# Loading the first attention's four head groups inside the projection before it

## The chip, the cores and the metric

The kernel runs on one core of one Trainium2 chip. The metric is the device time of one execution in microseconds. TensorE (PE), VectorE (DVE), ScalarE (ACT), GpSimd (POOL) and SyncE (SP) each run their own instruction stream; SP issues nearly all DMA transfers here, ACT issues a few.

## What is computed

Four blocks with residuals, on x of shape 4 x 1024 x 256. Only the first is touched by the change:

```
x = x + attention(layernorm(x))          # 16 heads of 16, ALiBi bias, causal
x = x + two layers of windowed attention and feed-forward
x = x + a selective scan (Mamba block)
x = x + a top-1 mixture of 32 experts
attention(h): qkv = h @ W_attn + b_attn; att = softmax(q k^T / 4 + alibi + causal); (att @ v) @ W_proj + b_proj
```

## The kernel before, in words

The program is a row of phases. A phase opens its own tiles and semaphores, lets the engines run their streams, and ends with a barrier of all engines at which its semaphores are cleared and its tiles freed. Phases hand data over through tensors in HBM (names `between_...`).

**`phase_qkv`, the projection (tiles `A_...`).** Eight chunks `c` of 512 tokens, two per sequence. For each chunk SP loads `x` (`load`, L255), DVE and POOL normalise it, TensorE transposes it and makes the q, k and value products, ACT puts the products of q and k out as bf16 (`parts`, L381), DVE takes the rest (`rest`, L336), and POOL splits the rest into a second and a third bf16 part (L299, L301). So q and k are each kept as three bf16 parts. `store(c)` on SP writes four value slices (`between_v`, L263) and six part tiles (`between_q_parts`, `between_k_parts`, L269) of 256 KB each. `parts` and `v` have two buffers: before ACT writes the parts of chunk c it waits on `qk_stored`, that is until the parts of chunk c-2 have landed in HBM. On SP the order is: load(c+3), store(c), next chunk. At the end SP waits for all stores, and the phase ends.

**`phase_attention` (tiles `B_...`).** 16 groups `g` = sequence x 4 head groups of four heads, with four buffers (`SETS`) for q, k and values. For a group, six blocks of 16 partitions are filled from the parts of q and six from the parts of k, partition blocks 0 to 95 (L630), rows 96 to 99 hold four extra rows (`q_rows`, `k_rows`), and `v_raw`, `centre` and `key_bias` follow: 17 transfers, about 1.93 MB (12 x 128 KB, 64 KB, 256 KB, 2 x 16 KB). Group 0 is loaded in two halves of its columns by `load_first`, q on SP (L608) and k on ACT (L871), and its values by `values(0)`. SP then issues load(1), load(2), then `put_shift(0)`, the weights, and enters the loop over groups, where load(g+3) comes ahead of what else the group needs.

For group 0 the order of work is strict. TensorE makes 48 score tiles (`p_max`, L911 and L914), DVE takes the maximum of each (L779), then turns them into a shift (L788 to L798), TensorE turns the shift (L935), ACT copies it to `shift_rows` (L880), and SP copies that into rows 96 to 99 of q by four transfers (`put_shift`, L639). Only then may TensorE make the scores that go into the exponential (`p_exp`, L947), with the maxima of the next group woven in between. From there on the shift of a group is made while the group before it is at work.

DVE casts `ident` and `future` at the start of the phase (L767 to L770); both TensorE and DVE wait for their two loads (L602), and TensorE waits for these casts.

`LocalAhead` is an object of the same kind as the new one: tiles of a later phase that are allocated early and loaded by the attention's SP stream.

Of the kernel before, what the change touches and what calls it, by code (L numbers as in the profile page):

```python
# [10 lines left out]
F32 = mybir.dt.float32  # L11
BF16 = mybir.dt.bfloat16
# [186 lines left out]

def phase_qkv(nc, T):
    with ExitStack() as ctx:
        a = Pool_(nc, ctx, "A")
        K = CHUNKS
# [45 lines left out]
        @block.sync  # L251
        def _(sp):
            def load(c):
                reached(sp, xn_ready, c - 2)
                sp.dma_start(x[:, c % 3, :, :], T["x"][c * CHUNK:(c + 1) * CHUNK, :].rearrange("(t p) d -> p t d", p=P)  # L255
                             ).then_inc(x_loaded[c % 3], 16)

            def store(c):
                u, seq, at = c % 2, c // PER_SEQ, c % PER_SEQ * CHUNK
                sp.wait_ge(v_ready, 2 * c + 2)  # L260
                for g in range(GROUPS):
                    row = seq * GROUPS * SEQ + g * SEQ + at
# [197 lines left out]
            "key_bias": seqs(key_bias), "future": np.stack([future, future.T.copy()]), "spread": spread}  # L460


def phase_attention(nc, T, local):
    with ExitStack() as ctx:
        a = Pool_(nc, ctx, "B")
        QB = SEQ // P
# [5 lines left out]
        FIRST = 4  # L472
        LEAD, TURN = 16, 36
        SCORES, PROBS = 3, 12
        SETS = 4
        KR = 100
        stream = [("turn", 0, 0), ("turn", 0, 1)]
        place = {}
        for g in range(NG):
# [11 lines left out]
        ident = a.sb("ident", [P, P])  # L491
        ident_b = a.sb("ident_b", [P, P], BF16)
        future = a.sb("future", [P, 2, P])
        future_b = a.sb("future_b", [P, 2, P], BF16)
        q = a.sb("q", [P, SETS, GH, SEQ], BF16)
        k = a.sb("k", [P, SETS, GH, SEQ], BF16)
        v_raw = a.sb("v_raw", [P, SETS, QB, GW])
        v = a.sb("v", [P, SETS, QB, GH, 32])
        centre = a.sb("centre", [P, SETS, QB * GH])
        key_bias = a.sb("key_bias", [P, SETS, 8, GH])  # L500
# [23 lines left out]
        fixed = a.sem("fixed")  # L524
        cast = a.sem("cast")
        loaded = [a.sem(f"loaded_{b}") for b in range(SETS)]
        v_ready = a.sem("v_ready")
        scored = a.sem("scored")
        maxed = a.sem("maxed")
# [21 lines left out]
        first_half = a.sem("first_half")  # L551
        second_half = a.sem("second_half")
        LOADED = 16 * 17
# [6 lines left out]
        def loaded_by(g):  # L560

            return LOADED * (g // SETS) + (LOADED if g % SETS else 48)

        def part_rows(g, part):
            at = g * GW + part * SEQS * DIM
            return slice(at, at + GW)

        def max_target(g, e):
            at = NE * g + e + 1
# [28 lines left out]

        @block.sync
        def _(sp):  # L600
            for dst, src in ((ident[:, :], T["ident"][:, :]), (future[:, :, :], T["future"].rearrange("a p n -> p a n"))):
                sp.dma_start(dst, src).then_inc(fixed, 16)  # L602

            def load_first():
                for half, done in ((0, first_half), (1, second_half)):
                    cols = slice(512 * half, 512 * half + 512)
                    for n, part in enumerate((0, 0, 1, 1, 0, 2)):
                        sp.dma_start(q[HD * n:HD * n + HD, 0, :, cols], T["q_parts"][part_rows(0, part), cols]  # L608
                                     .rearrange("(h d) t -> d h t", h=GH)).then_inc(done, 16)
                    if half == 0:  # L610
                        sp.dma_start(q[96:KR, 0, :, :], T["q_rows"]).then_inc(done, 16)
                values(0)

            def values(g):
                u = g % SETS
                sem = loaded[u]
                sp.dma_start(v_raw[:, u, :, :], T["v"][g * SEQ:(g + 1) * SEQ, :].rearrange("(t p) d -> p t d", p=P)
                             ).then_inc(sem, 16)
                sp.dma_start(centre[:, u, :], T["centre"][g:g + 1, :].broadcast_to([P, QB * GH])).then_inc(sem, 16)
                sp.dma_start(key_bias[:, u, :, :].rearrange("p a b -> p (a b)"), T["key_bias"][g * P:(g + 1) * P, :]  # L620
                             ).then_inc(sem, 16)

            def load(g):
                u = g % SETS
                sem = loaded[u]
                reached(sp, weighted, STEPS * (g - 3))
                for n, (q_part, k_part) in enumerate(((0, 0), (0, 1), (1, 0), (1, 1), (0, 2), (2, 0))):
                    for x, name, part in ((q, "q_parts", q_part), (k, "k_parts", k_part)):
                        at = g * GW + part * SEQS * DIM
                        sp.dma_start(x[HD * n:HD * n + HD, u, :, :], T[name][at:at + GW, :]  # L630
                                     .rearrange("(h d) t -> d h t", h=GH)).then_inc(sem, 16)
                sp.dma_start(k[96:KR, u, :, :], T["k_rows"][4 * g:4 * g + 4, :, :]).then_inc(sem, 16)
                sp.dma_start(q[96:KR, u, :, :], T["q_rows"]).then_inc(sem, 16)
                values(g)

            def put_shift(g):
                sp.wait_ge(exped, turned[g] + 1)
# [27 lines left out]
                sp.dma_start(T["z"][c * CHUNK + 1:(c + 1) * CHUNK + 1, :].rearrange("(t p) d -> p t d", p=P), z[:, c % 2, :, :]  # L665
                             ).then_inc(z_stored[c % 2], 16)

            load_first()
            load(1)
            load(2)  # L670
            put_shift(0)
            sp.dma_start(w[:, :, :], T["w_proj"].rearrange("(k p) n -> p k n", p=P)).then_inc(w_loaded, 16)
            sp.dma_start(bias[:, :], T["b_proj"].rearrange("(a n) -> a n", a=1).broadcast_to([P, DIM])).then_inc(w_loaded, 16)
            sp.dma_start(T["z"][0:1, :], T["zeros"][0:1, :]).then_inc(first_row, 16)
            for g in range(NG):
                if g + 3 < NG:
                    load(g + 3)
                i, at = divmod(g, GROUPS)
                if at == 2:
# [185 lines left out]

        @block.scalar
        def _(act):
            for half, done in ((0, first_half), (1, second_half)):
                cols = slice(512 * half, 512 * half + 512)
                for n, part in enumerate((0, 1, 0, 1, 2, 0)):  # L870
                    act.dma_start(k[HD * n:HD * n + HD, 0, :, cols], T["k_parts"][part_rows(0, part), cols]  # L871
                                  .rearrange("(h d) t -> d h t", h=GH)).then_inc(done, 16)
                if half == 0:
# [19 lines left out]
        def _(pe):  # L893
# [3 lines left out]
            def score(n):  # L897
# [2243 lines left out]

def build(nc, T):
    with nc.allow_non_contiguous_dma(reason="weights' columns, biases and slots, a few elements each"):
        phase_qkv(nc, T)
        with ExitStack() as outer:
            local = LocalAhead(nc, outer)
            phase_attention(nc, T, local)
            with ExitStack() as inner:
                feed = FeedAhead(nc, inner)
                for layer in range(2):  # L3150
                    phase_window(nc, T, layer, local, feed)
                    phase_feed_forward(nc, T, layer, layer == 1, feed, local)
        phase_front(nc, T)
        phase_scan(nc, T)
        phase_moe(nc, T)
# [21 lines left out]
```

## Time and profile before

| | us |
|---|---|
| median of 3 runs | 3643.21 |
| lowest, highest | 3635.83, 3643.5 |
| span of the profiled execution | 3631.7 |
| busy: PE, DVE, ACT, POOL | 3234.2, 2456.1, 1848.7, 1431.3 |
| projection, its last store landed | about 119 |
| attention, first instruction to first score for the exponential | 120.5 to 173.45 |

The span is counted from the first to the last instruction of the profiled execution; its own device time is not given apart from it. The median of the runs is 11.5 us above the span, and the lowest run 4.1 us above it. The change can move only what lies between the start and the first groups of the attention, so its effect can be read as a shift of a point in the timeline.

### The profile page before, as it was taken

How to read it: one execution, taken by the hardware profiler on the slowest of the kernel's cores; microseconds unless marked ns; L12 is line 12 of the kernel's file. 1: busy time of each engine (PE TensorE's matmuls, PEld its weight loads, DVE VectorE, ACT ScalarE, POOL GpSimd, SP SyncE). 2: the span in 40 equal slices, each digit the busy share in tenths (PEclk: the TensorE clock that was granted, in tenths of full speed). 3: DMA queues.
4: the chain of work that ended last, by engine and by line, in shares of the span. 5: the costliest groups of instructions: out<-in, count | busy, mean ns of one | idle time of the engine just before them, and what ended most of it. 6: DMA issues, size and time to landing. Idle time of an engine off the chain costs nothing. (4 is left out here: it accounts for less than half of the span.)

```text
span 3631.7 us, 52306 instructions
## 1 busy us (share of the span) xinstructions
PE 3234.2 (89%) x18096; PEld 1975.7 (54%) x18096; DVE 2456.1 (68%) x4653; ACT 1848.7 (51%) x3942; POOL 1431.3 (39%) x992
## 2 busy tenths in 40 slices
PE   8599999979999799999999899897388888887798
PEld 5244444346666555566666555332255565555676
DVE  8488887657777522377777232598599999996633
ACT  2177776836666411266666111366377777774100
POOL 4201111132222211132222111244699999995533
PEclk9699999989999899999999899998699999999899
DMA  5945676110020133000200221343615151512873
GB/s 169 161 62 88 78 99 123 28 38 23 23 65 23 51 133 96 22 23 25 67 23 17 69 69 39 101 159 130 240 59 204 58 204 59 203 58 98 296 226 117
DMA packets 276675, 347.29 MB, mean 96 GB/s; under 512 B 71168, under 2 KB 208368, under 8 KB 275772
## 3 DMA queue, kind: packets, MB, share of 16 engines
q1 hardware_dynamic: 261860, 308.29, 30.9%
q10 hardware_dynamic: 9432, 23.35, 1.9%
q0 software_dynamic: 5120, 12.30, 0.9%
q8 instruction: 145, 2.38, 0.3%
q14 instruction: 118, 0.97, 0.1%
HBM read 227.72 MB, written 112.80 MB: 94 GB/s over the span
## 5 line engine op out<-in xcount | busy, mean ns | idle before, releaser
L2373 POOL TENSOR_TENSOR H_feed<-H_ndu,H_bs 128x1024 f32<-128x1024 f32 x256 | 595.3, 2373 | 6.3 <-DMA H_bs<-between_bc 3.2
L888 ACT ACTIVATE B_probs<-B_p_exp,B_key_bias 128x512 f32<-128x512 f32 (+3 forms) x768 | 395.0, 582 | 162.6 <-PE B_p_exp L950 132.2
L779 DVE TENSOR_REDUCE B_part_max<-B_p_max 128x1 f32<-128x512 f32 (+3 forms) x768 | 374.5, 545 | 81.9 <-PE B_p_max L914 79.4
L1298 ACT ACTIVATE D_probs<-D_scores,D_neg,D_rq 128x256 f32<-128x256 f32 x512 | 283.1, 573 | 255.6 <-DVE D_neg L1219 255.6
L2344 ACT ACTIVATE H_decay<-H_ndt,H_rate 128x1024 f32<-128x1024 f32 x256 | 287.8, 1125 | 198.0 <-DVE H_turning L2426 103.2
L1658 PE MATMUL E_p_ag<-E_hT,FA_w 128*128 128x512 f32 x640 | 283.1, 602 | 1.9 <-ACT E_hT L1614 1.9
L911 PE MATMUL B_p_max<-B_k,B_q 100*128 100x512 bf16 (+3 forms) x768 | 256.9, 341 | 29.9 <-DMA B_q<-in_q_rows 20.0
L947 PE MATMUL B_p_exp<-B_q,B_k 100*128 100x512 bf16 (+3 forms) x768 | 250.6, 330 | 23.9 <-DMA B_q<-B_shift_rows 17.1
L2426 DVE TENSOR_TENSOR_SCAN H_turning<-H_decay,H_feed 128x1024 f32<-128x1024 f32 x112 | 253.5, 2274 | 24.1 <-POOL H_feed L2373 22.7
L2477 PEld LDWEIGHTS H_p_y<-H_minus,H_sT 128*128 128x128 f32 x1792 | 224.3, 199 | 76.2 <-ACT H_sT L2329 56.1
L2477 PE MATMUL H_p_y<-H_minus,H_sT 128*128 128x128 f32 x1792 | 232.6, 286 | 35.5 <-ACT H_sT L2329 35.5
L1156 POOL TENSOR_TENSOR D_rnorm<-D_norm,D_power 128x8 f32<-128x8 f32 x64 | 106.1, 1658 | 375.0 <-DVE D_norm L1174 375.0
L1630 ACT ACTIVATE E_gated<-E_p_ag,FA_b 128x512 f32<-128x512 f32 x96 | 62.6, 652 | 372.9 <-PE E_p_ag L1658 353.7
L2329 ACT ACTIVATE H_sT<-H_p_T,H_cT 128x128 f32<-128x128 f32 x896 | 242.9, 387 | 11.7 <-PE H_p_T L2467 11.4
L1353 PE MATMUL D_p_qk<-LA_wqkv,D_hT 128*128 128x512 f32 x512 | 242.3, 617 | 0.9 <-ACT D_hT L1273 0.9
L1216 DVE CUSTOM_DVE_ANT_0 D_scores<-D_scores,D_mask 128x256 f32<-128x256 f32 x512 | 201.9, 457 | 55.0 <-PE D_scores L1380 54.8
L2426 DVE TENSOR_TENSOR_SCAN H_decay<-H_decay,H_feed 128x1024 f32<-128x1024 f32 x96 | 218.9, 2280 | 15.5 <-POOL H_feed L2373 15.5
L1160 POOL TENSOR_TENSOR D_rnorm<-D_norm,D_power 128x8 f32<-128x8 f32 x64 | 106.7, 1667 | 287.7 <-DVE D_norm L1174 287.7
L1658 PEld LDWEIGHTS E_p_ag<-E_hT,FA_w 128*128 128x128 f32 x640 | 121.9, 192 | 155.3 <-issue 151.6
L1585 DVE SCALAR_TENSOR_TENSOR E_act_out<-E_p_ag,FA_b,E_gated 128x512 f32<-128x512 f32 x96 | 67.8, 706 | 198.7 <-ACT E_gated L1630 198.7
L2485 PE MATMUL H_p_y<-H_part,H_minus 128*128 128x512 f32 x384 | 184.5, 603 | 9.6 <-DVE H_part L2402 9.5
L911 PEld LDWEIGHTS B_p_max<-B_k,B_q 100*128 100x128 bf16 x768 | 75.3, 98 | 208.2 <-DVE B_part_max L779 131.4
(269 smaller groups left out, 6858.2 us busy)
## 6 DMA issues: line engine op xcount, KB each, us to landing
H_bs<-between_bc SPq DMA_DIRECT2D x64, 512.0 KB, 8.0
H_cs<-between_bc SPq DMA_DIRECT2D x36, 512.0 KB, 8.5
B_q<-between_q_parts SPq DMA_DIRECT2D x90, 128.0 KB
B_k<-between_k_parts SPq DMA_DIRECT2D x90, 128.0 KB
between_slots_x<-E_clear ACTq DMA_DIRECT2D x4, 2570.0 KB, 18.8
I_xe<-between_slots_x ACTq DMA_DIRECT2D x32, 257.0 KB, 3.9
LA_base<-between_z SPq DMA_DIRECT2D x64, 128.0 KB, 2.2
between_z<-D_z SPq DMA_DIRECT2D x64, 128.0 KB, 1.7
```

Source lines behind the costliest of these rows:

```text
L779: nc.vector.reduce_max(part_max[:, g % 2, kc, qb, h:h + 1], p_max[:, use % 3, 0:keys], AX.X).then_inc(maxed, 1)
L888: nc.scalar.activation(probs[:, x % PROBS, skip:512], p_exp[:, n % SCORES, skip:512], ACT.Exp, bias=key_bias[:, g % SETS, kb - 4 * Q + 4, ...
L911: last = nc.tensor.matmul(p_max[:, use % 3, 0:keys], q[0:KR, u, h, qb * P:(qb + 1) * P], k[0:KR, u, h, 512 * kc:512 * kc + keys], start=Tr ...
L947: last = nc.tensor.matmul(p_exp[:, n % SCORES, skip:512], k[0:KR, u, h, kb * P:(kb + 1) * P], q[0:KR, u, h, 512 * Q + skip:512 * Q + 512], ...
L1298: last = nc.scalar.activation(probs[:, place[m], :, :].rearrange("p a b -> p (a b)"), scores[:, place[m], :, :].rearrange("p a b -> p (a b ...
L1353: last = nc.tensor.matmul(p_qk[:, m, :], hT[:, i % 2, k, :], wqkv[:, k, m * INNER:(m + 1) * INNER], start=k == 0, stop=k == KD - 1)
L1658: last = nc.tensor.matmul(p_ag[:, m % 2, n, :], w1[:, k, at:at + P], hT[:, i % 2, k, :], **flags)
L2329: last = nc.scalar.activation(sT[:, k % 2, h * HB + b, :], p_T[:, h, b, :], ACT.Copy, scale=cT[:, i % 2, h * HB + b, s:s + 1])
L2344: nc.scalar.activation(decay[:, n % 2, :], ndt[:, g % 2, :], ACT.Exp, scale=rate[:, m, s:s + 1]).then_inc(decayed, 1)
L2373: nc.gpsimd.tensor_tensor(feed[:, n % AHEAD, :], ndu[:, g % 2, :], bs[:, s, :], ALU.mult).then_inc(fed, 1)
L2426: nc.vector.tensor_tensor_scan(out, decay[:, n % 2, :], feed[:, n % AHEAD, :], 0.0, ALU.mult, ALU.add).then_inc(scanned, 1)
L2477: last = nc.tensor.matmul(p_y[:, h, b * P:(b + 1) * P], sT[:, k % 2, h * HB + b, :], minus[:, :], start=False, stop=False)
```

## The change

The tiles q, k, v_raw, centre, key_bias, ident and future, with their semaphores, move into an object `AttentionAhead` (tiles `BA_...`), which is open during the projection too. The projection's SP stream loads the two fixed tables at its start and the four first groups after the stores of chunks 3, 4, 5 and 6. The attention's SP stream starts with `put_shift(0)`. Group 0 is no longer loaded in halves, ACT issues no transfer in the attention, and TensorE waits for all 17 transfers of group 0.

```diff
@@ phase_qkv, block.sync
             load(1)
             load(2)
+            first.load_fixed(sp, T)
             for c in range(K):
                 if c + 3 < K:
                     load(c + 3)
                 store(c)
+                if c == 3:
+                    for u in range(2):
+                        sp.wait_ge(qk_stored[u], 96)
+                        sp.wait_ge(v_stored[u], 16 * GROUPS)
+                if 3 <= c < 3 + first.SETS:
+                    first.load(sp, T, c - 3)
@@ new
+class AttentionAhead:
+    SETS, KR = 4, 100
+    LOADED = 16 * 17
...
+    def load_fixed(self, sp, T):
+        sp.dma_start(self.ident[:, :], T["ident"][:, :]).then_inc(self.fixed, 16)
+        sp.dma_start(self.future[:, :, :], T["future"].rearrange("a p n -> p a n")).then_inc(self.fixed, 16)
+
+    def load(self, sp, T, g):
+        u = g % self.SETS
+        sem = self.loaded[u]
+        for n, (q_part, k_part) in enumerate(((0, 0), (0, 1), (1, 0), (1, 1), (0, 2), (2, 0))):
+            for x, name, part in ((self.q, "q_parts", q_part), (self.k, "k_parts", k_part)):
+                at = g * GW + part * SEQS * DIM
+                sp.dma_start(x[HD * n:HD * n + HD, u, :, :], T[name][at:at + GW, :]
+                             .rearrange("(h d) t -> d h t", h=GH)).then_inc(sem, 16)
...
@@ phase_attention, block.sync
             def load(g):
-                u = g % SETS
-                sem = loaded[u]
-                reached(sp, weighted, STEPS * (g - 3))
...
+                sp.wait_ge(weighted, STEPS * (g - 3))
+                first.load(sp, T, g)
...
-            load_first()
-            load(1)
-            load(2)
             put_shift(0)
...
             for g in range(NG):
-                if g + 3 < NG:
+                if SETS <= g + 3 < NG:
                     load(g + 3)
@@ phase_attention, block.scalar
-            for half, done in ((0, first_half), (1, second_half)):
-                cols = slice(512 * half, 512 * half + 512)
-                for n, part in enumerate((0, 1, 0, 1, 2, 0)):
-                    act.dma_start(k[HD * n:HD * n + HD, 0, :, cols], ...)
-                if half == 0:
-                    act.dma_start(k[96:KR, 0, :, :], T["k_rows"][0:4, :, :]).then_inc(done, 16)
@@ phase_attention, block.tensor
-                if at == 0 and g:
+                if at == 0:
                     pe.wait_ge(loaded[u], loaded_by(g))
-                if n == 0:
-                    pe.wait_ge(first_half, 16 * 14)
-                if g == 0 and qb == QB // 2 and kc == 0 and h == 0:
-                    pe.wait_ge(second_half, 16 * 12)
@@ build
-        phase_qkv(nc, T)
         with ExitStack() as outer:
             local = LocalAhead(nc, outer)
-            phase_attention(nc, T, local)
+            with ExitStack() as early:
+                first = AttentionAhead(nc, early)
+                phase_qkv(nc, T, first)
+                phase_attention(nc, T, local, first)
```

## Rows read from the trace of the kernel before

**Rows 1.** The page: the span, and DMA's share in 40 slices.
```profile
span 3631.7 us, 52306 instructions
...
DMA  5945676110020133000200221343615151512873
```

**Rows 2.** Timeline from the attention's start to its first score for the exponential.
```profile
120.50 0.35 SPq L602 DMA_DIRECT2D B_ident<-in_ident  x1
...
124.63 0.23 DVE L767 CAST B_ident_b<-B_ident 128x128 bf16<-128x128 f32 x1 [13.71 <-DMA B_future<-in_future]
...
125.92 0.23 DVE L770 CAST B_future_b<-B_future 128x256 bf16<-128x256 f32 x1
...
130.17 0.26 PE L911 MATMUL B_p_max<-B_k,B_q 100*128 100x128 bf16 x1 [19.98 <-DMA B_q<-in_q_rows]
...
130.58 23.39 DVE L779 TENSOR_REDUCE B_part_max<-B_p_max 128x1 f32<-128x128 f32 x48 [4.43 <-PE B_p_max L914]
...
155.92 1.07 ACT L880 CAST B_shift_rows<-B_p_exp 128x512 bf16<-128x512 f32 x2 [48.45 <-PE B_p_exp L935]
...
160.16 2.61 SPq L639 DMA_DIRECT2D B_q<-B_shift_rows  x4
...
173.45 0.61 PE L947 MATMUL B_p_exp<-B_q,B_k 100*128 100x512 bf16 x1 [17.15 <-DMA B_q<-B_shift_rows]
```

**Rows 3.** Busy time by stretch; last columns: PE clock, DMA share, GB/s.
```profile
58.90:71.40 12.50, 11.41 (x41) 6.83 (x40) 12.22 (x19) 3.44 (x6) 7.18 (x4) 1.00 0.72 210
71.40:84.00 12.60, 11.48 (x42) 6.89 (x41) 12.32 (x19) 3.50 (x6) 7.19 (x4) 1.00 0.72 209
...
119.00:120.00 1.00, 0.00 (x0) 0.00 (x0) 0.00 (x0) 0.00 (x0) 0.00 (x0) 0.50 0.00 0
```

**Rows 4.** Waits from 60 to 120, and two timeline lines.
```profile
ACT A_parts L381 <- DMA between_k_parts<-A_parts: 23.7, 3, 8.5
...
92.38 2.55 ACT L381 ACTIVATE A_parts<-A_p_qk,A_bias_qk 128x512 bf16<-128x512 f32 x4 [7.45 <-DMA between_k_parts<-A_parts]
...
96.39 2.71 DVE L336 SCALAR_TENSOR_TENSOR A_rest<-A_p_qk,A_bias_qk,A_parts 128x512 f32<-128x512 f32 x4
```

**Rows 5.** SP's timeline: chunk 3's stores, the last x, the last store.
```profile
71.42 2.07 SPq L263 DMA_DIRECT2D between_v<-A_v  x4
...
78.00 0.73 SPq L255 DMA_DIRECT2D A_x<-in_x  x1
...
116.13 0.73 SPq L269 DMA_DIRECT2D between_k_parts<-A_parts  x1
```

**Rows 6.** DMA issues: KB each, median us to landing; 250 to 270, 0 to 120.
```profile
B_x<-in_x SPq DMA_DIRECT2D x1, 512.0 KB, 11.2
...
A_x<-in_x SPq DMA_DIRECT2D x8, 512.0 KB, 4.7
...
between_v<-A_v SPq DMA_DIRECT2D x32, 128.0 KB, 2.3
...
B_yT<-B_yn SPq DMA_DIRECT2D x6, 32.0 KB, 4.9
```

**Rows 7.** Group 5's load: first issue, then stretches as in rows 3.
```profile
250.83 0.33 SPq L630 DMA_DIRECT2D B_q<-between_q_parts  x1
...
251.00:266.00 15.00, 14.78 (x122) 6.38 (x121) 13.26 (x30) 12.24 (x25) 2.45 (x3) 1.00 1.03 121
...
267.00:268.00 1.00, 1.00 (x10) 0.39 (x12) 1.00 (x3) 1.00 (x3) 0.00 (x0) 1.00 1.23 260
```

**Rows 8.** POOL's timeline: copies that wait for all transfers of groups 0 and 1.
```profile
138.71 0.61 POOL L714 COPY B_v<-B_v_raw 128x512 f32<-128x512 f32 x1 [15.39 <-DMA B_key_bias<-in_key_bias]
156.64 0.61 POOL L714 COPY B_v<-B_v_raw 128x512 f32<-128x512 f32 x1 [17.31 <-DMA B_key_bias<-in_key_bias]
```

**Rows 9.** Stretches as in rows 3: from chunk 3's last store on.
```profile
78.00:119.50 41.50, 29.95 (x105) 18.02 (x103) 26.22 (x35) 9.40 (x14) 23.03 (x9) 0.95 0.79 232
116.00:119.00 3.00, 0.00 (x0) 0.00 (x0) 0.00 (x0) 0.00 (x0) 0.00 (x0) 0.50 0.98 333
```

**Rows 10.** Stretches as in rows 3: group 0's halves, the first exponentials.
```profile
124.00:128.00 4.00, 0.00 (x0) 0.00 (x0) 1.36 (x4) 0.00 (x0) 0.00 (x0) 0.50 1.15 196
...
176.00:180.00 4.00, 4.00 (x25) 2.04 (x23) 2.02 (x6) 2.82 (x5) 0.00 (x0) 0.52 1.10 124
180.00:184.00 4.00, 4.00 (x40) 1.91 (x33) 2.76 (x6) 1.94 (x5) 0.00 (x0) 1.00 1.25 122
```

More of the change, by code:

```diff
@@ L195, in normalise, with phase_qkv @@
                                        ALU.subtract, ALU.mult)
-def phase_qkv(nc, T):
+def phase_qkv(nc, T, first):
     with ExitStack() as ctx:
@@ L460, in attention_tables, with __init__, loaded_by, phase_attention @@
             "key_bias": seqs(key_bias), "future": np.stack([future, future.T.copy()]), "spread": spread}
-def phase_attention(nc, T, local):
+class AttentionAhead:
+    SETS, KR = 4, 100
+    LOADED = 16 * 17
+    def __init__(self, nc, ctx):
+        sb = lambda name, shape, dt=F32: ctx.enter_context(nc.sbuf_tensor(f"BA_{name}", shape, dt))
+        qb = SEQ // P
+        self.ident = sb("ident", [P, P])
+        self.future = sb("future", [P, 2, P])
+        self.q = sb("q", [P, self.SETS, GH, SEQ], BF16)
+        self.k = sb("k", [P, self.SETS, GH, SEQ], BF16)
+        self.v_raw = sb("v_raw", [P, self.SETS, qb, GW])
+        self.centre = sb("centre", [P, self.SETS, qb * GH])
+        self.key_bias = sb("key_bias", [P, self.SETS, 8, GH])
+        self.fixed = nc.alloc_semaphore("BA_fixed")
+        self.loaded = [nc.alloc_semaphore(f"BA_loaded_{b}") for b in range(self.SETS)]
+    def loaded_by(self, g):
+        return self.LOADED * (g // self.SETS + 1)
+    def load_fixed(self, sp, T):
[9 more added lines that the diff above has]
+                             .rearrange("(h d) t -> d h t", h=GH)).then_inc(sem, 16)
+        sp.dma_start(self.k[96:self.KR, u, :, :], T["k_rows"][4 * g:4 * g + 4, :, :]).then_inc(sem, 16)
+        sp.dma_start(self.q[96:self.KR, u, :, :], T["q_rows"]).then_inc(sem, 16)
+        sp.dma_start(self.v_raw[:, u, :, :], T["v"][g * SEQ:(g + 1) * SEQ, :].rearrange("(t p) d -> p t d", p=P)
+                     ).then_inc(sem, 16)
+        sp.dma_start(self.centre[:, u, :], T["centre"][g:g + 1, :].broadcast_to([P, SEQ // P * GH])).then_inc(sem, 16)
+        sp.dma_start(self.key_bias[:, u, :, :].rearrange("p a b -> p (a b)"), T["key_bias"][g * P:(g + 1) * P, :]
+                     ).then_inc(sem, 16)
+def phase_attention(nc, T, local, first):
     with ExitStack() as ctx:
@@ L474, in phase_attention @@
         SCORES, PROBS = 3, 12
-        SETS = 4
-        KR = 100
+        SETS, KR = first.SETS, first.KR
         stream = [("turn", 0, 0), ("turn", 0, 1)]
@@ L490, in phase_attention @@
         tail_units = [(SEQS - 1, 2), (SEQS - 1, 3)]
-        ident = a.sb("ident", [P, P])
+        ident, future, q, k, v_raw = first.ident, first.future, first.q, first.k, first.v_raw
+        centre, key_bias, fixed, loaded, loaded_by = first.centre, first.key_bias, first.fixed, first.loaded, first.loaded_by
         ident_b = a.sb("ident_b", [P, P], BF16)
-        future = a.sb("future", [P, 2, P])
         future_b = a.sb("future_b", [P, 2, P], BF16)
-        q = a.sb("q", [P, SETS, GH, SEQ], BF16)
-        k = a.sb("k", [P, SETS, GH, SEQ], BF16)
-        v_raw = a.sb("v_raw", [P, SETS, QB, GW])
         v = a.sb("v", [P, SETS, QB, GH, 32])
-        centre = a.sb("centre", [P, SETS, QB * GH])
-        key_bias = a.sb("key_bias", [P, SETS, 8, GH])
         part_max = a.sb("part_max", [P, 2, 2, QB, GH])
@@ L523, in phase_attention @@
         p_acc = a.ps("p_acc", [P, 2, 512])
-        fixed = a.sem("fixed")
         cast = a.sem("cast")
-        loaded = [a.sem(f"loaded_{b}") for b in range(SETS)]
         v_ready = a.sem("v_ready")
@@ L558, in reached @@
                 eng.wait_ge(sem, value)
[L560 to L566, printed above, removed]
         def max_target(g, e):
@@ L600, in _ @@
         def _(sp):
-            for dst, src in ((ident[:, :], T["ident"][:, :]), (future[:, :, :], T["future"].rearrange("a p n -> p a n"))):
-                sp.dma_start(dst, src).then_inc(fixed, 16)
-            def load_first():
-                for half, done in ((0, first_half), (1, second_half)):
-                    cols = slice(512 * half, 512 * half + 512)
-                    for n, part in enumerate((0, 0, 1, 1, 0, 2)):
-                        sp.dma_start(q[HD * n:HD * n + HD, 0, :, cols], T["q_parts"][part_rows(0, part), cols]
-                                     .rearrange("(h d) t -> d h t", h=GH)).then_inc(done, 16)
-                    if half == 0:
-                        sp.dma_start(q[96:KR, 0, :, :], T["q_rows"]).then_inc(done, 16)
-                values(0)
-            def values(g):
-                u = g % SETS
-                sem = loaded[u]
[L617 to L621, printed above, removed]
-            def load(g):
-                u = g % SETS
-                sem = loaded[u]
-                reached(sp, weighted, STEPS * (g - 3))
[L627 to L634, printed above, removed]
+            def load(g):
+                sp.wait_ge(weighted, STEPS * (g - 3))
+                first.load(sp, T, g)
             def put_shift(g):
@@ L867, in _ @@
         def _(act):
-            for half, done in ((0, first_half), (1, second_half)):
-                cols = slice(512 * half, 512 * half + 512)
-                for n, part in enumerate((0, 1, 0, 1, 2, 0)):
-                    act.dma_start(k[HD * n:HD * n + HD, 0, :, cols], T["k_parts"][part_rows(0, part), cols]
-                                  .rearrange("(h d) t -> d h t", h=GH)).then_inc(done, 16)
-                if half == 0:
-                    act.dma_start(k[96:KR, 0, :, :], T["k_rows"][0:4, :, :]).then_inc(done, 16)
             for n, (kind, g, at) in enumerate(stream):
```

3 lines of the change are left out of this document (removed).

## The prediction

> **What bounds the kernel now.** I first read the page for the span and for DMA's row over the slices: the first two slices, 0 to 182 us, are among the busiest for DMA [rows 1]. Every other phase keeps its code, so I looked only at these. The question is what has to end before the first score for the exponential at 173.45 [rows 2], because from there on the attention runs as it did.
>
> In the projection, busy time by chunk shows DVE at 12.2 of 12.5 us; a chunk takes 12.5 us because DVE is full. DMA is busy 0.72 of that time at 210 GB/s [rows 3]. So DMA has about 0.28 x 12.5 = 3.5 us to spare per chunk. The waits show that ACT waits 7 to 8 us per chunk for the stores of two chunks earlier, 23.7 us in three waits, which costs nothing now: the parts of chunk 6 start at 92.38, and DVE comes to them at 96.39, some 4 us of slack [rows 4]. The last store is issued at 116.13 [rows 5] and DMA is still by 119.0 [rows 3]; the attention's first instruction is at 120.5.
>
> From 120.5 to 173.45 one thing follows another [rows 2]. TensorE waits for the group's first half until 130.17. DVE's 48 maxima then take 23.4 us and bound that stage, whatever TensorE's clock is. The shift is turned and its copy by ACT ends at 156.99 (155.92 + 1.07). But the copy into q's rows is issued only at 160.16, since SP is held up issuing groups 1 and 2, and its data then lie behind group 2: TensorE starts at 173.45, 13.3 us after the issue, of which the four issues themselves are 2.6.
>
> **What the change removes.** Count from the end of the projection, E (119.0 before). The barrier takes 1.5 (119.0 to 120.5) as before. The two tables are there already, so DVE's casts and memsets, 124.63 to 126.15, start at once: 1.5. TensorE starts 0.3 later: first score at E + 3.3, where it was E + 11.2. That is 7.9 gained. From the first score to the copy's end, 130.17 to 156.99, stays 26.8. The shift rows' issue follows at once: 3.2 gained. They land on an empty queue. For this the trace has no clean row in this place; the bounds are the value stores' landing of 2.3 after an issue and the 4.9 of the yT copies, which have the same form [rows 6], each behind 2.6 us of issuing, so 4.9 to 7.5. I take the lower, as the rows are 8 KB each: 8.4 gained. Together 7.9 + 3.2 + 8.4 = 19.5 us, if E stays at 119.0. ACT's 13 issues go as well; ACT is idle there for 48.45 us [rows 2] and nothing is gained. The new wait of TensorE for all 17 transfers of group 0, and those of ACT, DVE and POOL, are over before the phase starts, since group 0 has landed long before E.
>
> **What it adds.** Two table loads (192 KB) between load(2) and load(3): under 1 us of SP and of DMA, hidden, because x of chunk 3 is read some 30 us later. Then 4 x 17 = 68 issues, at some 0.43 us each about 8 us of SP per group, and their transfers. Group 0's are issued at 78.0, where SP has done store(3) [rows 5]; the wait for chunks 0 and 1 put ahead of them is over by then. Behind them on SP's stream and in its queue stand load(7) and store(4); behind group 1 stands store(5), behind group 2 store(6), behind group 3 store(7). And E is the landing of store(7).
>
> What does a group cost on the queue? Group 5's load is issued from 250.83, into a nearly empty queue, and DMA moves 121 GB/s at a share of 1.03 until the 512 KB of x behind it come through at 267, at 260 GB/s: 16.3 us [rows 7]. Groups 0 and 1 land 17.9 us apart [rows 8], and group 2 and the shift rows come 16.8 us after group 1 (156.64 to 173.45). I take 16.5 for 1.93 MB, that is 117 GB/s. It is not the issuing that limits it (8 us) but the transfers: a busy share over 1 at a third of the 333 GB/s that the stores reach when they have the queue to themselves [rows 9].
>
> Do transfers behind it wait? The x load issued at 259.01, behind group 5, landed after 11.2 us, against a median of 4.7 in the projection [rows 6]; it began to move when the group was through [rows 7]. So I add the times in order.
>
> From 78.0 to 119.5 DMA is busy 0.79 of 41.5 us [rows 9], 32.8 us of work: the rest of store(3), load(7), and the stores of chunks 4 to 7. With the four groups it is 32.8 + 66.0 = 98.8 us, against 41 before, and the queue stays full: store(c)'s landing lets chunk c+2 go on, whose own stores are ready some 15 us later, less than the group and the store that lie between. So E = 78.0 + 98.8 = 176.8, in place of 119.0: 57.8 later. Chunks 6 and 7 are late on the way: store(4) lands at about 105 and not at 92.38, which uses up the 4 us of slack [rows 4]; this costs nothing more, as DMA is the bound then and not DVE.
>
> **The sum.** 57.8 lost, 19.5 gained: the first score for the exponential at 173.45 + 38.3 = 211.8. What comes after is the same: group 3 and the weights were loaded under TensorE's work before. The first 6.5 us of exponentials ran at the lower clock (0.52 from 176 to 180, then 1.00) after a time in which TensorE idled [rows 10]; it will have idled about 5 us and not 17, so at best 3 us come back. I take none. On the profiled execution: 3631.7 + 38.3 = 3670.0. The median of the runs is 11.5 above that span, so 3643.2 + 38.3 = 3681.5; I say 3681.
>
> Bounds of the likeliest case: a group at 15.3 (some store traffic slipping in at the borders, four times 1.2) and the stores at 333 GB/s, which makes 9.6 MB (232 x 41.5) 28.9 us, and 3 us of clock, give +26.6 or so; a group at 17.9 and a slow landing give +38.3 + 5.6 + 2.6 = +46.5. Its own range is 3669 to 3690.
>
> **Rivals.**
> *The loads hide (faster).* Load and store have different directions, the projection has spare DMA time, and a group might trickle in beside the stores. Then E stays at 119.0 and all of 19.5 is gained: 3624. For it speaks that ACT has slack. Against it: four groups need 66 us, and the spare time from 78 to 119 is 41 - 32.8 = 8 us. It comes out faster than before only when a group costs the queue less than (41 - 32.8 + 19.5) / 4 = 6.9 us. At the stores' rate of some 300 GB/s a group takes 6.4 us, which gives E = 78 + 32.8 + 25.6 = 136.4, 17.4 later and -2.1 in sum: 3641. No load of this shape comes near that rate. Chances: 0.05 for the first, 0.05 for the second. The Trainium skill speaks for the change here (DMA: Bandwidth & Descriptors, Rules for kernel authors): issue the DMA early, do compute, wait late, and the setup overlaps. By that rule the sum would be the 19.5 gained; the trace agrees for the copy's own wait, but the rule does not say what stands behind the early transfer.
>
> *Partial overlap (slower, by less).* When q's halves went by SP's queue and k's by ACT's, 196 GB/s were moved from 124 to 128 [rows 10], so engines and memory can do more than 121 with different destinations in flight. If loads and stores mix so, a group costs 1.93 MB at 190, 10.2 us: E = 78 + 32.8 + 40.8 = 151.6, 32.6 later, +13.1 in sum: 3656. Against it: here one queue issues both, and x behind group 5 did not mix. Chance 0.12. The Trainium skill has a rule that points this way (DMA: Bandwidth & Descriptors, Two DMAs through the same engine are not ordered): descriptors start in order but are pipelined, with reading and writing as separate queues. By it a store may overlap the end of a load; the trace shows at most a microsecond or so of that per border [rows 7].
>
> *Something more goes wrong (slower by over 47).* The stalls of SP on a full queue delay stores that are ready, and DMA runs dry at times. Each of the four borders could cost 3 us, the time of a store's landing: 3693. Chance 0.06. The likeliest case has 0.72.
>
> **How the numbers follow.** A measurement of this kernel tells a change from none at about 0.2%, 7 us. Faster holds the hidden case and a little of the one at 3641: 0.06. Same holds the rest of that: 0.05. Slower: 0.89. The range runs from the partial overlap's 3654 to 3692 and leaves out the two cases without loss and part of the worst.
>
> **What would show it.** In the profile after: SP's issues of chunk 7's stores end near 170 and not at 117, or later than 150 at least; ACT's waits for `between_k_parts` in chunks 6 and 7 grow to over 15 us; DMA's share is near 1 from 80 until the projection's end; the attention's first score comes 3.3 us after that end; shift rows are issued right after ACT's copy and TensorE starts about 5 us later. It is wrong if the group loads run above 200 GB/s beside the stores, if E lies before 140, or if the later groups' timeline is not shifted as a whole.

## The result and the profile after

The changed kernel takes 3668.9 us (median of 4 runs, 3666.27 to 3676.0) against 3640.5 for the kernel before (median of 4, 3635.83 to 3643.5): ratio 1.0096, 95% interval 1.0082 to 1.011. It is slower: by 35 us by this ratio, by 28.4 us by the two medians, whose quotient is 1.0078. With four runs each the two don't agree better than that. 3681 with 3654 to 3692 had been forecast. The profiled execution has a span of 3668.1 us and took 3669.89, 1.8 us more.

SP's timeline in the projection of the changed kernel: group 0's first transfer, the last x, the value stores behind each of the four groups, the last store, and the shift rows. It answers to [rows 2, 5].

```profile
77.48 0.58 SPq L502 DMA_DIRECT2D BA_q<-between_q_parts  x1
...
85.78 0.43 SPq L255 DMA_DIRECT2D A_x<-in_x  x1
86.25 10.52 SPq L263 DMA_DIRECT2D between_v<-A_v  x4
...
109.36 9.52 SPq L263 DMA_DIRECT2D between_v<-A_v  x4
...
131.09 10.34 SPq L263 DMA_DIRECT2D between_v<-A_v  x4
...
153.65 10.22 SPq L263 DMA_DIRECT2D between_v<-A_v  x4
...
166.90 0.73 SPq L269 DMA_DIRECT2D between_k_parts<-A_parts  x1
200.31 2.63 SPq L639 DMA_DIRECT2D BA_q<-B_shift_rows  x4
```

Four value stores take SP 10 us behind each group and 2.07 where nothing lies before them [rows 5]. I read this as SP standing at a full queue; the trace shows only how long the issues took. The last store is issued at 166.90 and not at 116.13.

Busy time by stretch (last columns: PE clock, DMA share, GB/s), as in [rows 3, 9]:

```profile
84.00:88.00 4.00, 4.00 (x17) 2.95 (x17) 0.71 (x2) 0.40 (x1) 0.00 (x0) 1.00 1.11 122
88.00:92.00 4.00, 2.23 (x6) 0.69 (x4) 0.00 (x0) 0.00 (x0) 0.00 (x0) 1.00 1.11 121
...
136.00:140.00 4.00, 0.00 (x0) 0.00 (x0) 0.00 (x0) 0.00 (x0) 0.00 (x0) 0.50 1.30 94
...
164.00:168.00 4.00, 0.00 (x0) 0.00 (x0) 0.00 (x0) 0.00 (x0) 0.00 (x0) 0.50 1.15 342
168.00:172.00 4.00, 0.00 (x0) 0.00 (x0) 0.61 (x1) 0.00 (x0) 0.65 (x1) 0.50 0.45 153
...
77.00:170.00 93.00, 32.27 (x106) 18.78 (x104) 26.58 (x36) 9.28 (x14) 23.39 (x10) 0.72 1.13 188
```

Read the last line first. Over 93 us DMA is busy without a gap (share 1.13 in the mean, and over 1 in every 4 us up to 168), and DVE only 26.6 of 93, where it had been 12.2 of 12.5 [rows 3]. The bound of the projection has moved from DVE to DMA. Within it stretches of 121 GB/s (a group) and of over 320 (stores) take turns. With the engines idle, as from 136 to 140, only DMA is left.

The waits that grew, and the attention's first stage (DVE, ACT and PE timelines), as in [rows 2, 4]:

```profile
97.95 1.41 DVE L323 BATCH_NORM_STATS2 A_stats<-A_x 128x6 f32<-128x256 f32 x4 [13.24 <-DMA A_x<-in_x]
...
104.19 2.42 ACT L388 ACTIVATE A_parts<-A_p_qk,A_bias_qk 128x512 bf16<-128x512 f32 x4 [19.80 <-DMA between_k_parts<-A_parts]
...
125.73 2.42 ACT L388 ACTIVATE A_parts<-A_p_qk,A_bias_qk 128x512 bf16<-128x512 f32 x4 [15.47 <-DMA between_k_parts<-A_parts]
...
171.35 1.80 POOL L703 MEMSET B_v<- 128x2048 f32 x1 [36.02 <-POOLq L83]
...
173.42 0.29 PE L897 MATMUL B_p_max<-BA_k,BA_q 100*128 100x128 bf16 x1 [50.43 <-DVE B_future_b L767]
...
173.85 23.41 DVE L776 TENSOR_REDUCE B_part_max<-B_p_max 128x1 f32<-128x128 f32 x48 [0.49 <-PE B_p_max L900]
...
199.22 1.07 ACT L870 CAST B_shift_rows<-B_p_exp 128x512 bf16<-128x512 f32 x2 [71.07 <-PE B_p_exp L921]
...
204.28 0.61 PE L933 MATMUL B_p_exp<-BA_q,BA_k 100*128 100x512 bf16 x1 [4.67 <-DMA BA_q<-B_shift_rows]
```

What the change was to remove is removed: the first score comes 2.1 us after the phase's first instruction (it was 9.7), the shift rows are issued 0.02 us after ACT's copy, and the wait for them is 4.67 us where it was 17.15. All of it happens 51 us later, since the phase starts at 171.35 and not at 120.5. The first score for the exponential moves from 173.45 to 204.28, 30.8 us.

From there the attention runs nearly as it did: the copies of the shift rows of groups 2 to 11 are issued 30.1 us later than before, every one. Its last transposition of an output starts at 733.0 before and at 763.9 after (operations on one tile, first and last start):

```profile
L801 DVE STREAM_TRANSPOSE B_zt<-B_p_acc x32: 703/706/717, 223.4 to 763.9; 128x512 f32<-128x512 f32 x32
```

So 30.9 us are the change's. The rest of the 36.4 between the two spans, 5.5 us, arises in the later phases, whose code is the same. The experiments say what most of it is.

### The profile page after: what moved, and what is told of

Same layout as the page of the kernel before. It is cut to its first block and busy times, and to the rows that moved or that the text cites. A ratio compares the mean times of both kernels' runs of the same rounds, so it can differ in the third digit from the quotient of the medians.

```text
span 3668.1 us, 52295 instructions
## 1 busy us (share of the span) xinstructions
PE 3238.6 (88%) x18096; PEld 1977.5 (54%) x18096; DVE 2457.4 (67%) x4653; ACT 1846.7 (50%) x3942; POOL 1430.6 (39%) x992
## 5 line engine op out<-in xcount | busy, mean ns | idle before, releaser
L878 ACT ACTIVATE B_probs<-B_p_exp,BA_key_bias 128x512 f32<-128x512 f32 (+3 forms) x768 | 394.2, 582 | 150.8 <-PE B_p_exp L936 120.2
L897 PE MATMUL B_p_max<-BA_k,BA_q 100*128 100x512 bf16 (+3 forms) x768 | 256.7, 341 | 60.5 <-DVE B_future_b L767 50.4
L933 PE MATMUL B_p_exp<-BA_q,BA_k 100*128 100x512 bf16 (+3 forms) x768 | 250.1, 330 | 11.4 <-ACT B_probs L878 6.4
L2315 ACT ACTIVATE H_sT<-H_p_T,H_cT 128x128 f32<-128x128 f32 x896 | 242.3, 387 | 13.8 <-PE H_p_T L2453 13.6
L2412 DVE TENSOR_TENSOR_SCAN H_decay<-H_decay,H_feed 128x1024 f32<-128x1024 f32 x96 | 218.9, 2280 | 16.0 <-POOL H_feed L2359 15.9
L897 PEld LDWEIGHTS B_p_max<-BA_k,BA_q 100*128 100x128 bf16 x768 | 75.2, 98 | 238.2 <-DVE B_part_max L776 133.0
## 6 DMA issues: line engine op xcount, KB each, us to landing
between_slots_x<-E_clear ACTq DMA_DIRECT2D x4, 2570.0 KB, 19.5
```

The lines of the kernel that those rows point to most:

```text
L878: nc.scalar.activation(probs[:, x % PROBS, skip:512], p_exp[:, n % SCORES, skip:512], ACT.Exp, bias=key_bias[:, g % SETS, kb - 4 * Q + 4, ...
L933: last = nc.tensor.matmul(p_exp[:, n % SCORES, skip:512], k[0:KR, u, h, kb * P:(kb + 1) * P], q[0:KR, u, h, 512 * Q + skip:512 * Q + 512], ...
L2315: last = nc.scalar.activation(sT[:, k % 2, h * HB + b, :], p_T[:, h, b, :], ACT.Copy, scale=cT[:, i % 2, h * HB + b, s:s + 1])
L2412: nc.vector.tensor_tensor_scan(out, decay[:, n % 2, :], feed[:, n % AHEAD, :], 0.0, ALU.mult, ALU.add).then_inc(scanned, 1)
```

## The experiments

A measurement of the whole is worth some 5 us here. A point of the timeline is worth more: from group 2 to group 11 the issue of the shift rows keeps its distance from before within 0.1 us in every kernel. So each experiment is read at the attention's first instruction (120.50 before), its first score for the exponential, those shift rows, and its last output transposition.

| kernel | first instruction | first score for exp | shift rows, groups 2 to 11, against before | last transposition, against before | ratio, 95% interval |
|---|---|---|---|---|---|
| before | 120.5 | 173.5 | | 733.0 | |
| the change | 171.4 | 204.3 | +30.1 | +30.9 | 1.0096 (1.0082 to 1.011) |
| shift rows first | 120.3 | 159.9 | -13.8 | -9.3 | 0.9961 (0.9948 to 0.9973) |
| three groups ahead | 157.4 | 190.3 | +14.8 | +12.4 | 1.0053 (1.0038 to 1.0067) |
| one group ahead | 135.0 | 167.7 | -8.2 | -8.9 | 0.9981 (0.997 to 0.9992) |
| one group, spread | 124.3 | 157.2 | -17.0 | -18.0 | 0.9969 (0.9959 to 0.998) |
| four groups, ACT's queue | 151.0 | 183.9 | +9.7 | +9.2 | 1.0019 (1.0005 to 1.0032) |
| other order of blocks | 167.9 | 200.8 | +27.2 | +27.2 | 1.0062 (1.0043 to 1.008) |
| spare loads, 16 partitions | 158.4 | 211.4 | +37.9 | +37.0 | 1.0095 (1.0077 to 1.0112) |
| spare loads, 128 partitions | 137.5 | 193.5 | +20.7 | +22.9 | 1.0044 (1.0028 to 1.0059) |
| one group, x first | 129.8 | 162.7 | -11.1 | -10.4 | 0.9981 (0.9972 to 0.999) |
| four groups, x first | 171.1 | 203.8 | +28.3 | +29.2 | 1.0094 (1.0079 to 1.011) |
| one group, spread earlier | 121.0 | 153.9 | -19.7 | -20.3 | 0.9955 (0.9942 to 0.9969) |

The two columns against before differ by up to 4.5 us, and this arises in one place, after group 11. There the eight transfers of `yT` stand on SP's queue behind the load of group 14, 512 KB of x and tiles of the later phase, and TensorE stands idle ahead of the output projection, which by the code waits for them. SP and PE timelines of before, of shift rows first, and the PE line of three groups ahead:

```profile
577.39 9.21 SPq L651 DMA_DIRECT2D B_yT<-B_yn  x8
588.05 3.75 PE L927 MATMUL B_p_max<-B_w,B_yT 128*128 128x256 f32 x8 [4.29 <-issue]
...
566.22 11.16 SPq L651 DMA_DIRECT2D B_yT<-B_yn  x8
578.83 3.67 PE L927 MATMUL B_p_max<-B_w,B_yT 128*128 128x256 f32 x8 [8.82 <-issue]
...
600.73 3.49 PE L913 MATMUL B_p_max<-B_w,B_yT 128*128 128x256 f32 x8 [2.13 <-issue]
```

So the kernel had a second place where urgent transfers stand behind bulky ones. In every kernel the two columns differ as this idle time does, to within 0.6 us. The profile names no releaser for the wait, and no experiment moved these transfers.

**The half of the change that needs no load: shift rows first.**

```diff
--- before
             load(1)
-            load(2)
             put_shift(0)
+            load(2)
```

> The kernel before, with the shift rows of group 0 issued ahead of group 2's load. Queue theory (what is issued earlier on SP delays what stands behind it by its own DMA time): the copy is issued at 157.0, group 1 has landed at 156.6, so the first score for the exponential comes at about 162 and not at 173.45, and nothing else moves: 11 us faster than before, ratio 0.997. Rival (the 17 us wait is only handed on to groups 2 and 3, which now land some 5 us later): no change.

The copy is issued at 155.98 and the exponential starts at 159.9, 13.5 us earlier (162 had been expected; 1.1 us were gained already at the first score, 129.12 for 130.17, ahead of the swapped lines). Nothing is handed on to groups 2 and 3: up to group 11 all shift rows come 13.8 us earlier. At the attention's end 9.3 are left, and the 4.5 us between are the idle time above, 8.82 us for 4.29. SP and ACT timelines:

```profile
155.98 2.61 SPq L639 DMA_DIRECT2D B_q<-B_shift_rows  x4
158.63 0.44 SPq L630 DMA_DIRECT2D B_q<-between_q_parts  x1
...
160.68 2.18 ACT L888 ACTIVATE B_probs<-B_p_exp,B_key_bias 128x512 f32<-128x512 f32 x3 [4.73 <-PE B_p_exp L950]
```

By the timeline two swapped lines gain 9.3 us; the whole kernel's ratio of 0.9961 says 10 to 19. The wait of 17.15 us fell to 4.66 by SP's order alone.

**How many groups.** Three groups ahead, and one, with the others loaded in the attention in the order load(1), shift rows, load(2), load(3) in the loop. In the loop of both, a load waits as it did in the kernel before (`reached`).

```diff
--- after, three groups
-                if 3 <= c < 3 + first.SETS:
+                if 3 <= c < 6:
...
-                if SETS <= g + 3 < NG:
+                if g + 3 < NG:
--- after, one group
-                if 3 <= c < 3 + first.SETS:
+                if c == 3:
                     first.load(sp, T, c - 3)
...
+            load(1)
             put_shift(0)
+            load(2)
...
-                if SETS <= g + 3 < NG:
+                if g + 3 < NG:
```

> The changed kernel with three groups loaded in the projection and group 3 in the attention's loop as before. Queue theory: the projection ends 16 us earlier than in the changed kernel, near 154, and the whole is 15 us slower than before (ratio 1.004) in place of 31 to 36. Rival (the loss lies in the late phases or in something that is there once, whatever the number of groups): over 25 us slower than before.

> The changed kernel with only group 0 loaded in the projection, in one piece after chunk 3's stores; in the attention load(1), the shift rows, load(2), and load(3) in the loop. Queue theory: one group of 16 us ahead of store(4) holds chunk 6 back by about 12 us, of which 4 are slack, so the projection ends 8 us later, at 127; the 20 us gained behind it stay: 12 us faster than before, ratio 0.997. Rival (each group in the projection costs its full 16 us): 4 us faster at most.

Without the fourth group the attention starts 14.0 us earlier (157.4 for 171.4), although the first group went out 1.2 us later (78.71 for 77.48): near the 16 of the queue theory. The loss falls from 30.1 to 14.8 at groups 2 to 11; at the attention's end it falls from 30.9 to 12.4, of which some 3 us are TensorE's idle time shown above. With a single group the attention starts at 135.0 and the projection ends near 133.5, not at the 127 expected: one group costs 14.5 us, nearly its full time, so the rival was right in this. At the attention's end 8.9 us are gained; 12 had been expected, and 4 at most by the rival. The DVE timeline shows the place:

```profile
84.72 1.39 DVE L343 SCALAR_TENSOR_TENSOR A_rest<-A_p_qk,A_bias_qk,A_parts 128x512 f32<-128x512 f32 x2
99.63 1.41 DVE L323 BATCH_NORM_STATS2 A_stats<-A_x 128x6 f32<-128x256 f32 x4 [13.51 <-DMA A_x<-in_x]
```

I had counted the slack of ACT's wait for store(4) and not that load(7), which stands behind the group as well, is wanted by DVE at once. In this kernel DMA then idles (share 0.19 from 104 to 108, 0.03 to 112), because the projection waits for itself.

**The x first.** To try this, load(7) goes ahead of group 0, with one group and with four.

```diff
--- one group ahead, and the change itself
-                if c + 3 < K:
+                if c + 3 < K and c != 4:
                     load(c + 3)
                 store(c)
                 if c == 3:
+                    load(7)
```

> One group ahead in one piece, but the last chunk of x is loaded before the group and not behind it. In the trace of one group ahead the projection's last q and k products end 14.4 us later than before, because DVE waits for that x until the group is through. If this wait is what one group costs beyond its DMA time, the projection now ends some 4 to 8 us earlier and the first score for the exponential comes near 160 to 163 and not at 167.7. Rival (the wait of ACT for store(4), which also stands behind the group, is as late): no change against 167.7.

> The changed kernel with the same edit, all four groups ahead. If DMA's total work bounds the projection there, this moves nothing: first score for the exponential at 204, 31 us later than before. Rival (the wait for x bounds it there too): 4 to 8 us earlier than 204.

With one group the attention starts 5.1 us earlier and the exponential at 162.7 for 167.7. The rest, 9.3 us against before, I put down to ACT's wait for store(4), 19.7 us at the longest, through which DVE waits 8.9 us for ACT's parts. With four groups the exponential starts at 203.8 for 204.3: nothing. DMA bounds there, and who waits for it makes no difference. Both came as expected.

**Who issues.** The four groups are issued by ACT, after its copies for chunks 3 to 6.

```diff
--- after, block.scalar of phase_qkv (and the same lines out of block.sync)
                 if c + 1 < K:
                     put_xT(c + 1)
+                if c == 3:
+                    for b in range(2):
+                        act.wait_ge(qk_stored[b], 96)
+                        act.wait_ge(v_stored[b], 16 * GROUPS)
+                if 3 <= c < 3 + first.SETS:
+                    first.load(act, T, c - 3)
```

> The changed kernel with the four groups' loads issued by ACT in the projection, after its copies for chunks 3 to 6; all else as changed. Queue theory in its strict form (the stores wait because they stand behind the loads in SP's own queue): stores and loads now share the engines, the projection ends at 125 to 140 and not at 170, the groups go on landing in the attention; 5 to 15 us faster than before. Rival (capacity: all 63 us of loads have to be moved before the stores end, whoever issues them): as the changed kernel, 30 us slower than before.

Neither theory holds. The projection does not end at 125 to 140, but near 149.5, with all groups landed (DMA's share is 0.35 from 149 to 150 and 0.00 behind it); nor at 170. Nearly the same bytes as in the change (17.2 MB for 17.5 in the windows) need 74 us and not 93:

```profile
76.00:150.00 74.00, 38.96 (x112) 21.58 (x112) 31.72 (x47) 10.70 (x17) 26.28 (x12) 0.78 1.09 232
```

232 GB/s against 188. So in one queue a group holds the stores up by its full time; in two queues, loads and stores run partly beside each other. It is the partial overlap of the prediction's second rival, which is there to be had, but not by issuing on SP. SP's issues are not free of the loads even so: its four value stores take 9.37 us at 89.47 and 13.96 at 120.98. ACT pays too: its longest wait for stores is 21.2 us. The Trainium skill (DMA: Bandwidth & Descriptors, Rules for kernel authors) says that spreading DMAs over the issuing engines does not help bandwidth; for this mix the two windows above differ by a fifth, and the measurement decides. It is one kernel against one; the order in which transfers go out changed with the queue.

**Why a group takes 16 us.** Three kernels. In one the neighbours in the queue fill blocks far apart. In the two others the kernel before gets 4 x 12 more transfers of 128 KB, in the places of the change, into a tile that nothing reads; the transfers are into 16 partitions each, or into all 128.

```diff
--- after, other order of blocks
-        for n, (q_part, k_part) in enumerate(((0, 0), (0, 1), (1, 0), (1, 1), (0, 2), (2, 0))):
-            for x, name, part in ((self.q, "q_parts", q_part), (self.k, "k_parts", k_part)):
+        pairs = ((0, 0), (0, 1), (1, 0), (1, 1), (0, 2), (2, 0))
+        for n, m in ((0, 4), (1, 5), (4, 0), (5, 1), (2, 3), (3, 2)):
+            for x, name, n, part in ((self.q, "q_parts", n, pairs[n][0]), (self.k, "k_parts", m, pairs[m][1])):
...
--- before, 16 partitions
+    sp.dma_start(spare[HD * n:HD * n + HD, side, g, :, :], T[name][at:at + GW, :].rearrange("(h d) t -> d h t", h=GH))
--- before, 128 partitions
+    sp.dma_start(spare[:, side, g, n // 2, 512 * (n % 2):512 * (n % 2) + 512], T[name][at:at + GW, :].rearrange("r (a t) -> (r a) t", a=2))
```

> The changed kernel with the twelve transfers of a group in another order: neighbours in the queue fill partition blocks that lie far apart (0 to 15 beside 64 to 79, and so on), in place of q and k into the same block. If the 121 GB/s come from neighbours that meet at the same partitions, the groups get faster, 10 to 13 us each in place of 16, and the projection ends 12 to 24 us earlier. If they come from each single transfer reaching 16 partitions only, nothing changes: about 30 to 36 us slower than before, as the changed kernel.

> The kernel before, with 4 x 12 transfers of q and k parts added in the projection at the places of the change, into a tile that nothing reads, each into 16 partitions as the real loads. Queue theory: 1.57 MB at 121 GB/s are 13.0 us per group, so the projection ends at 77.4 + 28.9 + 52 = 158, about 39 us later, and nothing is gained behind it: ratio 1.0107. Rival (transfers fill idle DMA time): under 20 us slower.

> The same added transfers of 128 KB each from the same parts, but each into all 128 partitions (1 KB rows in place of 2 KB). If the rate of a load is set by its 16 partitions, these move at the 300 GB/s of the stores, 5.2 us per group, and the projection ends near 128 to 132: 9 to 13 us slower than before, ratio 1.003. If it is set by bytes or by reading what was just written, 39 us slower as with 16 partitions.

The order of the blocks is worth 3.5 us in all four groups together: neighbours that meet are a small part. With 16 partitions the projection ends at 156.85 (158.35 less the barrier's 1.5). The first of the transfers goes out at 78.40, and 28.9 us are what the stores and the last x need at 333 GB/s (9.6 MB). So the four sets cost (156.85 - 78.4 - 28.9) / 4 = 12.4 us each, 127 GB/s, near the 13.0 expected. With 128 partitions they go out from 78.80 and the projection ends at 136.0: at most (136.0 - 78.8 - 28.9) / 4 = 7.1 us each, 222 GB/s or more, for the same bytes from the same place. It is not the 5.2 expected: DMA was not always busy (share 0.69 from 100 to 104), and DVE waited for x here too, 4.8 us. The whole stretch with 128 partitions, 278 GB/s:

```profile
78.00:136.00 58.00, 33.48 (x107) 20.29 (x105) 27.29 (x36) 9.61 (x14) 23.65 (x10) 0.83 0.94 278
```

And with 16, 199 GB/s, with a stretch in which the added transfers alone run:

```profile
80.00:157.00 77.00, 30.24 (x101) 17.88 (x99) 24.27 (x35) 9.39 (x14) 21.16 (x9) 0.75 1.10 199
...
140.00:148.00 8.00, 0.00 (x0) 0.00 (x0) 0.00 (x0) 0.00 (x0) 0.00 (x0) 0.50 1.09 124
```

So the shape of the destination makes the group dear, not its bytes and not reading what was just written. The rows are 1 KB with 128 partitions and 2 KB with 16, so partitions and row length changed together, and these runs don't tell them apart. The Trainium skill (SBUF — State Buffer, Door 1: The DMA port swizzle) says that a transfer's bandwidth goes by how many of 16 ports its partitions reach, and gives 104 GB/s for partitions 0 to 15 against 328 for all. The runs agree in kind (124 to 127 against 222 or more); their 124 lies above its figure. In the wide case the attention ends 22.9 us later and not the 17.0 by which it starts later. Of these 6 us, 2.8 are a longer wait for the first shift rows (19.95 us for 17.15), and 2.3 the idle time ahead of the output projection (6.55 for 4.29).

**A version that keeps the gain.** Group 0 only, in pieces that fit what a chunk leaves idle.

```diff
--- after, spread (steps yields after each of the 12 transfers, and once for the last five)
-                if c == 3:
+                if c == 2:
                     for u in range(2):
                         sp.wait_ge(qk_stored[u], 96)
                         sp.wait_ge(v_stored[u], 16 * GROUPS)
-                if 3 <= c < 3 + first.SETS:
-                    first.load(sp, T, c - 3)
+                    steps = first.steps(sp, T, 0)
+                if 2 <= c < 7:
+                    for _ in range(3):
+                        next(steps, None)
--- spread earlier: the wait and four steps ahead of store(2), then
+                if 2 <= c < 5:
+                    for _ in range(3):
+                        next(steps, None)
```

> As one group ahead, but group 0's transfers go out three at a time after the stores of chunks 2 to 6. Queue theory: three transfers of 128 KB are 3.3 us of DMA, which fits the 3.5 us that a chunk leaves idle, so the projection still ends at 119 to 122 and 17 to 20 us are gained, ratio 0.995. Rival (loads beside the stores cost more than their time alone, or SP's issues are what counts): no better than one group in one piece.

> Group 0 spread as before, but four transfers ahead of chunk 2's stores and three after those of chunks 2, 3 and 4, none after chunk 4, where DMA is busy without a gap until the projection's end. Each piece fits a gap, so the projection ends at 119 to 121 in place of 122.7, and the first score for the exponential comes at 154 to 156, 18 to 20 us earlier than before; ratio 0.995 to 0.997. Rival (earlier pieces delay the stores that DVE's buffers wait for): later than 157.2.

Spread, a group costs 3.8 us of the projection (first instruction at 124.3) in place of 14.5; the projection ends 0.8 us past the 119 to 122 expected. Spread earlier, it costs 0.5 us, as expected, and the attention gains 20.3 us. Spread earlier, busy time by stretch where the projection ends, and the first exponentials:

```profile
118.00:119.00 1.00, 0.00 (x0) 0.00 (x0) 0.00 (x0) 0.00 (x0) 0.00 (x0) 0.50 1.01 348
119.00:120.00 1.00, 0.00 (x0) 0.00 (x0) 0.00 (x0) 0.00 (x0) 0.00 (x0) 0.50 0.40 135
...
154.62 2.18 ACT L888 ACTIVATE B_probs<-B_p_exp,BA_key_bias 128x512 f32<-128x512 f32 x3 [4.72 <-PE B_p_exp L946]
```

It takes 3617.05 us (median of 5) against 3635.06, ratio 0.9955: faster than both kernels. By the whole kernel's time it can't be told from the two swapped lines (0.9961, the intervals overlap); by the timeline it gains 20.3 against 9.3.

**The later phases.** In every profile the last output is 0.6 to 8.5 us later, against before, than its attention alone would make it: 5.4 with two swapped lines, 5.6 for the change, 0.6 for one group ahead, 4.7 in the mean of the twelve. The size does not follow what was changed. The kernel before itself took 3627.81 to 3641.47 us in 15 runs on one chip. Each of these is one profile against the same one of before, which was on the quick side: its span of 3631.7, with the 1.8 us found for the changed kernel, makes 3633.5, below all four of its runs (3635.83 to 3643.5). The many runs of each kernel don't share this profile. By their ratios the whole kernels moved by 6.9 us less to 6.9 us more than the last transposition did, 0.9 us more in the mean. So I take most of the 5.5 us for scatter, and not for a cost of the change; repeated profiles of before, which would show it directly, were not made.

## Why the prediction was right

**The mechanism.** It was forecast that four groups on SP's queue would hold back the stores behind them, that the projection would end by DMA's total work, and that all savings behind it would come and be outweighed. The profile shows each link, and the counts of three and one group take it apart.

**The end of the projection.** Forecast 176.8; it was 171.35 - 1.5 = 169.85, 6.9 us earlier. The term that was mis-sized is DMA's work from 78.0 on. I had taken share times window, 32.8 us; but the 9.6 MB need 28.9 us when the queue is full and the stores run at the 333 GB/s of [rows 9], which I had kept for the lower bound only. That is 3.9, if the stores ran at that rate here too (342 GB/s from 164 to 168). A group then came to (169.85 - 77.48 - 28.9) / 4 = 15.9 us and not 16.5: 2.5 in all. It fits the 121 GB/s of the stretches, 16.0 us for 1.93 MB. The first group went out 0.5 earlier.

**The gains behind it.** Forecast: 35.1 us from the projection's end to the first score for the exponential (176.8 to 211.9), where it was 54.45. It was 34.4: 3.6 to the first score (3.3), 26.9 of maxima and turning (26.8), 4.0 for the rows to land (4.9). The gain is 20.0 and not 19.5. Of the 3 us that the clock might give back at best, at most 0.7 are seen, between the first score for the exponential (30.8 later) and group 2 (30.1 later).

**The sum.** 50.85 lost, 20.0 gained, 30.8; forecast 38.3. The bounds, +26.6 to +46.5, held it. That the span was forecast to within 2 us (3670.0, and 3668.1 measured) is luck in part: the 7.5 us too many met 5.5 us of later phases that nobody had forecast. The 3681 for the median is 12.6 too high before rounding. It stood on 38.3 us where the medians moved by 28.4, which is 9.9 of it. The other 2.7 are the starting point, 3643.2, the median of three runs, where four gave 3640.5; the 11.5 us between that median and the span were not a fixed distance, since a profiled execution takes only 1.8 us more than its span.

**The rivals.** Loads that hide: no, with four groups; with one, in pieces, they do, and the trace had shown the room (3.5 us per chunk). Partial overlap: not in one queue; in two, yes. Something more going wrong: SP does stand at a full queue, 10 us per group, as forecast, but DMA never ran dry up to 168, so it cost nothing.

**What I missed without harm.** The wait of DVE for the last x, 13.24 us, where I had named only the one of ACT for store(4). Under four groups DMA hid it. In the forecast for one group it was the larger part (5.1) of the 6.5 us by which I was off, 133.5 for 127.

## What to carry to other kernels

In these runs a prefetch in one piece cost nearly its own transfer time to everything that was issued behind it on the same queue. So add it up against the idle share of DMA in that stage, not against the idle time of the engine that would have waited. If it doesn't fit, move only what the next stage needs first, in pieces as large as the gaps, and behind what the present stage waits for. And look at the order of issue before the place of the loads: two lines swapped gave, by the timeline at the attention's end, nearly half the gain of the best version, and seven tenths of it (13.8 us of 19.7) up to group 11. Then look for the next place of the same kind: what the swap gained was in part lost again at the `yT` transfers, which stand behind a bulky load as the shift rows had.

## What the runs showed of the hardware

- Loads and stores of nearly the same bytes, all on SP's queue, took 93 us at 188 GB/s; with the loads on ACT's queue 74 us at 232 GB/s.
- 48 transfers of 128 KB into 16 partitions each (rows of 2 KB) moved at 124 to 127 GB/s; into 128 partitions each (rows of 1 KB), at 222 or more.
- SP's own issues took longer behind a bulky load: four value stores took 9.5 to 10.5 us behind each group of 17 transfers, 2.1 to 3.9 behind twelve transfers into 128 partitions, and 2.07 with nothing before them.
